# Normalising and projecting by pairs of row blocks, a new order for the last groups, and one branch less at the end of a differential attention and FFN kernel

## The reference

```python
xn = layernorm(x)                                   # (1, 1024, 256)
# attention: 16 heads, d = 8 for queries and keys, 16 for values, causal
q1, k1, q2, k2, v = split(xn @ Wqkv)                # 128, 128, 128, 128, 256 columns
diff = softmax(q1 k1') v - lam * softmax(q2 k2') v  # lam from four vectors of 8
diff = 0.44.. * diff / sqrt(mean(diff**2) + 1e-5)   # per head and row
attn = diff.reshape(...) @ Wproj
# FFN, operands cast to fp8, results bf16
ffn = fp8(gelu(fp8(xn) @ fp8(Wg[0])) * (fp8(xn) @ fp8(Wg[1]))) @ fp8(Wlin)   # hidden 1024
return x + attn + ffn
```

## Time and profile before

| what | us |
|---|---|
| median of 3 runs (lowest, highest) | 199.3 (198.45, 199.69) |
| the profiled execution | 199.27 |
| its span, first to last instruction | 197.5 |
| first exponential starts | 38.0 |
| last exponential starts | 178.9 |
| last product with the values ends (the transpose behind it starts) | 182.9 |
| last block of the output copied by VectorE | 190.4 |

### The profile page before, as it was taken

One profiled execution on the slowest core, in us unless ns is written; L12 is line 12 of the kernel. 1 busy time (PEld: TensorE's weight loads), 2 busy tenths in 40 slices (PEclk: granted clock), 3 DMA queues, 4 the chain that ended last, 5 costly groups with the idle time before them and its releaser, 6 DMA issues.

```text
span 197.5 us, 3554 instructions
## 1 busy us (share of the span) xinstructions
PE 182.2 (92%) x1446; PEld 78.3 (40%) x1450; DVE 92.4 (47%) x218; ACT 163.6 (83%) x136; POOL 59.4 (30%) x71
## 2 busy tenths in 40 slices
PE   6899989899999999999989999999998999899940
PEld 6855334454332323242333424344342423233830
DVE  0975798431223240540472025216703697895840
ACT  2156865899999999999999999999999899998010
POOL 8526600042216142314442043235216124320000
PEclk9999999999999999999999999999999999999997
DMA  5967377780000000000277781000000000000051
GB/s 174 404 242 245 73 179 205 207 190 10 0 0 3 0 0 3 0 0 3 60 203 188 181 191 39 0 3 0 0 3 0 0 3 0 0 3 0 0 178 44
DMA packets 8149, 14.99 MB, mean 76 GB/s; under 512 B 1984, under 2 KB 5312, under 8 KB 8128
## 3 DMA queue, kind: packets, MB, share of 16 engines
q1 hardware_dynamic: 7440, 14.05, 25.5%
q10 hardware_dynamic: 688, 0.66, 1.0%
HBM read 5.26 MB, written 1.05 MB: 32 GB/s over the span
## 4 chain that ended last, share of the span: by engine, by line
PE 74%; ACT 15%; DVE 4%; POOL 1%; issue 1%; POOLq 0%; DVEq 0%
PE ps L910 29%; PE ps L898 17%; ACT probs L442 13%; PE ps L752 8%; PE ps L758 4%; PE ps L941 4%; PE ps L747 3%; PE ps L851 3%; PE ps L813 3%; DVE area L529 2%; DVE o_t L594 1%; ACT probs L430 1%; PE ps L742 1%; PE ps L947 1%; ACT L430 1%
## 5 line engine op out<-in xcount | busy, mean ns | idle before, releaser
L442 ACT ACTIVATE probs<-ps,shift 128x1536 f32<-128x1536 f32 x96 | 140.1, 1554 | 2.4 <-PE ps L898 1.6
L910 PE MATMUL ps<-probs,v_all 128*32 128x512 f32 (+3 forms) x768 | 78.1, 496 | 1.5 <-DVE o_t L594 1.5
L366 POOL TENSOR_SCALAR_AFFINE_SELECT probs<-probs 128x1024 f32<-128x1024 f32 (+1 forms) x40 | 36.7, 917 | 109.7 <-ACT probs L442 109.6
L898 PE MATMUL ps<-q_st,k_st 32*128 32x512 f32 (+3 forms) x384 | 49.8, 420 | 1.2 <-issue 0.8
L898 PEld LDWEIGHTS ps<-q_st,k_st 32*128 32x128 f32 x384 | 22.4, 182 | 58.6 <-ACT probs L442 30.4
L594 DVE STREAM_TRANSPOSE o_t<-ps 128x512 f32<-128x512 f32 x16 | 11.5, 717 | 49.5 <-PE ps L910 49.5
L910 PEld LDWEIGHTS ps<-probs,v_all 128*32 128x32 f32 x768 | 16.4, 108 | 19.6 <-issue 13.9
L752 PE MATMUL ps<-xn_t,w_q 128*128 128x512 f32 (+1 forms) x38 | 17.3, 557 | 0.8 <-ACT xn_t L393 0.8
L813 PE MATMUL ps<-area 128*128 128x512 fp8e4 x64 | 14.5, 379 | 1.0 <-DVE area L529 1.0
L430 ACT ACTIVATE probs<-ps 128x512 bf16<-128x512 f32 x16 | 9.3, 597 | 4.5 <-PE ps L813 2.7
L529 DVE TENSOR_TENSOR area<-ps,probs 128x512 fp8e4<-128x512 f32 x16 | 10.5, 687 | 1.8 <-ACT probs L430 1.7
(11 more groups left out here) (78 smaller groups left out, 117.2 us busy)
## 6 DMA issues: line engine op xcount, KB each, us to landing
q_st<-parts SPq DMA_DIRECT2D x32, 128.0 KB, 2.8
k_st<-parts SPq DMA_DIRECT2D x32, 128.0 KB, 2.8
probs<-L_ffn_w_gating SPq DMA_DIRECT2D x4, 512.0 KB, 7.8
probs<-L_ffn_w_linear SPq DMA_DIRECT2D x1, 1024.0 KB, 13.1
w_q<-L_attn_Wqkv SPq DMA_DIRECT2D x2, 384.0 KB, 5.8
out<-probs SPq DMA_DIRECT2D x3, 256.0 KB, 3.0
x_sb<-L_attn_x SPq DMA_DIRECT2D x2, 256.0 KB, 4.2
x_sb<-L_attn_x ACTq DMA_DIRECT2D x2, 256.0 KB, 4.5
```

The source lines that it names most:

```text
L366: pool.affine_select(out=blocks, in_=blocks, pattern=pattern, compare_op=ALU.is_ge, fill=0.0, base=0, channel_multiplier=-1).then_inc(mask ...
L442: act.activation(probs[:, at:at + PER_UNIT, :].rearrange("p s u -> p (s u)"), ps[:, 3 * (n % 2):3 * (n % 2) + 3, :].rearrange("p b n -> p ...
L898: ins = pe.matmul(ps[:, bank, at:at + wide * P], k_st[rows, g % STACKS, kb * P:(kb + 1) * P], q_st[rows, g % STACKS, queries], start=True, ...
L910: ins = pe.matmul(ps[32 * j:32 * j + 32, 6, q0 % HALF:q0 % HALF + wide * P], v_all[:, g % HG, kb, 32 * j:32 * j + 32], probs[:, slot + j, ...
```

## The change

1. **Start.** `stats_of`, `root`, `transposes` and `turned` work on pairs of blocks, four times. Of each pair VectorE normalises the even block and ScalarE the odd one (`odd_block`). A pair is transposed into one bank. TensorE's order is: pair 0; half of unit 0; pair 1; half of unit 1; the other halves of units 0 and 1; pair 2; values of block 0; pair 3; values of block 1; first norms; unit 2 and so on. WARM_UP is unchanged.
2. **Chunks.** Chunks 5 and 6 change places, so that the masked one is complete two units earlier.
3. **Lateness.** `due` uses 5 for groups 0 to 4, 4 for group 5, 3 for group 6; for group 7 it uses 3, and 2 from chunk 6 on. Before: 5 for groups 0 to 5, 4 for group 6, 3 or (chunks 5 to 8) 2 for group 7.
4. **Second FFN layer.** Block 2 moves to slot 53, block 3 to slots 56 and 57, block 4 to slot 61, and the others one slot ahead.
5. **Output projection.** project(0, 0) and project(1, 0) move from slot 94 to slots 83 and 87. `ending` begins with a wait for out_t_ready 3 and project(0, 1) and (1, 1), ahead of chunks 7 and 8; then blocks 2 and 3 whole, and the first halves of 4 to 7 ahead of the wait for out_t_ready 4. The Y_BANK table follows; blocks 4 and 5 share a bank, and VectorE adds their residual.
6. **VectorE's order.** `take` stands by itself and is placed ahead of other work; `inverse_root` comes in pieces of 64, 32, 16 and 16 columns; the first `down` is ahead of the last `keep`. ScalarE loads the table for the square root by a small operation behind the last exponential, and copies blocks 2, 3 and 6.
7. **Branches.** The flag of the second branch is 0 or 2; the general second branch exists once on TensorE, and behind second_branch(False) one jump is left.

```diff
-    [(1, 4, 512)], [(7, 1, 896), (5, 3, 640)], [(2, 4, 512)], [(3, 4, 512)],
+    [(7, 1, 896), (5, 3, 640)], [(1, 4, 512)], [(2, 4, 512)], [(3, 4, 512)],
...
-DIAGONALS = {0: [0], 1: [0, 128], 2: [0, 256], 4: [0], 6: [0, 128]}
+DIAGONALS = {0: [0], 1: [0, 128], 2: [0, 256], 4: [0], 5: [0, 128]}
...
-DOWN_AT = {44: (0, 0, 4), 45: (0, 4, 8), 49: (1, 0, 8), 56: (2, 0, 4), 57: (2, 4, 8), 61: (3, 0, 8), 65: (4, 0, 8),
-           68: (5, 0, 4), 69: (5, 4, 8), 73: (6, 0, 8), 79: (7, 0, 4), 80: (7, 4, 8)}
+DOWN_AT = {44: (0, 0, 4), 45: (0, 4, 8), 49: (1, 0, 8), 53: (2, 0, 8), 56: (3, 0, 4), 57: (3, 4, 8), 61: (4, 0, 8),
+           67: (5, 0, 4), 68: (5, 4, 8), 72: (6, 0, 8), 78: (7, 0, 4), 79: (7, 4, 8)}
+
+Y_AT = {83: 0, 87: 1}
...
+    late = (5, 5, 5, 5, 5, 4, 3, (3, 3, 3, 3, 3, 3, 2, 2)[min(c, 7)])[g]
     return g * STEPS + last_unit(c) + late
...
             root(0)
+            odd_block(0)
+            root(1)
             turned(0)
-            root(1)
+            odd_block(1)
+            root(2)
+            turned(1)
+            odd_block(2)
+            root(3)
             upper(0)
+            odd_block(3)
+            upper(1)
+            turned(2)
             square_of(0)
-            upper(1)
-            turned(1)
+            turned(3)
...
-            down(0)
+            take(4, 0)
             own.step(difference(0, 0))
             down(1)
+            take(4, 1)
             own.step(difference(0, 1))
+            take(5, 0)
             own.step(difference(1, 0))
             down(2)
+            take(5, 1)
             own.step(difference(1, 1))
-            own.step(difference(2, 0))
+            take(6, 0)
+            inverse_root(slice(0, 64))
             down(3)
-            inverse_root(slice(0, 64))
             scale_by_root(0, all_of)
             scale_by_root(1, all_of)
             turn_back(0, 0)
             turn_back(0, 1)
+            own.step(difference(2, 0))
+            take(6, 1)
             own.step(difference(2, 1))
+            inverse_root(slice(64, 96))
+            take(7, 0)
+            scale_by_root(2, all_of)
             own.step(difference(3, 0))
-            inverse_root(slice(64, 112))
-            scale_by_root(2, all_of)
+            inverse_root(slice(96, 112))
             scale_by_root(3, first)
             turn_back(1, 0)
+            add(0)
+            take(7, 1)
             difference(3, 1).then_inc(ms_ready, 1)
...
             transposes(0)
             pe.wait_ge(wq_in, 32)
-            unit(0)
-            unit(1)
-            transposes(1)
+
+            for i in range(2):
+                pe.wait_ge(xt_out, i + 1)
+                for u in range(2):
+                    for k in range(KC):
+                        ins = queries_keys(u, QK_BANK[u], k, i * C, C)
+                    if i == 1:
+                        ins.then_inc(qk_ready, 1)
+                    elif u == 0:
+                        transposes(1)
+            transposes(2)
+            project_values(0, 6)
+            transposes(3)
+            project_values(1, 6)
...
             def ending():
 
+                pe.wait_ge(out_t_ready, 3)
+                project(0, 1)
+                project(1, 1).then_inc(y_ready, 1)
                 values_due(UNITS, 0, GROUPS)
+                values_due(UNITS + 1, 0, GROUPS)
+                pe.wait_ge(res_ready, TB // 2)
                 for b in (2, 3):
                     project(b, 0)
-                values_due(UNITS + 1, 0, GROUPS)
-                pe.wait_ge(out_t_ready, 3)
-                for b in range(4):
-                    project(b, 1)
-                pe.wait_ge(res_ready, TB // 2)
-                for b in range(4, TB):
+                    residual(b)
+                    project(b, 1).then_inc(y_ready, 1)
+                for b in (4, 5, 7, 6):
                     project(b, 0)
-                    residual(b)
+                residual(6)
                 pe.wait_ge(out_t_ready, 4)
-                for b in range(4, TB):
-                    project(b, 1)
+                project(4, 1)
+                for b in (5, 6, 7):
+                    project(b, 1).then_inc(y_ready, 1)
...
+            pe.reg_load(mode, flag[0:1, 0:1])
+            with pe.If_eq(mode, 0):
                 attention(0, False)
                 pe.wait_ge(flag_ready, 2)
...
+                pe.reg_load(mode, flag[0:1, 1:2])
+                with pe.If_eq(mode, 0):
                     second_branch(False)
...
+            with pe.If_ne(mode, 0):
+                with pe.If_eq(mode, 1):
+                    attention(0, True)
+                    pe.wait_ge(flag_ready, 2)
+                    pe.reg_load(mode, flag[0:1, 1:2])
+                    with pe.If_eq(mode, 0):
+                        second_branch(False)
+                with pe.If_eq(mode, 2):
                     second_branch(True)
```

More of the change, by code:

```diff
@@ L298, in _ @@
             sp.wait_ge(flag_ready, 2)
-            large2 = sp.value_load(flag[0:1, 1:2], min_val=0, max_val=1)
-            with sp.If(large2 == 1):
+            large2 = sp.value_load(flag[0:1, 1:2], min_val=0, max_val=2)
+            with sp.If(large2 == 2):
                 sp.wait_ge(max_split[1], 1)
@@ L385, in _, with root, odd_block, turned @@
                 act.dma_start(x_sb[:, b:b + 2, :], x_rows[:, b:b + 2, :]).then_inc(x_in[b // 2], 16)
[L386 to L394, removed]
+            def root(i):
+                act.wait_ge(var_ready, i + 1)
+                act.activation(rstd[:, 1, 2 * i:2 * i + 2], rstd[:, 0, 2 * i:2 * i + 2], ACT.Sqrt).then_inc(root_ready, 1)
+            def odd_block(i):
+                b = 2 * i + 1
+                act.wait_ge(moved_ready, i + 1)
+                act.activation(xn[:, b, :], x_sb[:, b, :], ACT.Identity, bias=rstd[:, 3, b:b + 1],
+                               scale=rstd[:, 2, b:b + 1]).then_inc(odd_ready, 1)
+            def turned(i):
+                act.wait_ge(xt_ready, i + 1)
+                act.activation(xn_t[:, :, i * C:(i + 1) * C], ps[:, i, :].rearrange("p (k n) -> p k n", k=KC), ACT.Copy
+                               ).then_inc(xt_out, 1)
             def upper(u):
@@ L608, in difference @@
                 b, s = slice(16 * h, 16 * h + 16), slice(32 * i + 16 * h, 32 * i + 16 * h + 16)
-                take(HG + i, h)
                 divide(HG + i, h)
@@ L687, in _ @@
             keep(3, 0)
-            keep(3, 1)
             dve.wait_ge(flag_ready, 2)
-            with dve.If(dve.value_load(flag[0:1, 1:2], min_val=0, max_val=1) == 1):
+            large2 = dve.value_load(flag[0:1, 1:2], min_val=0, max_val=2)
+            steps = own.n
+            with dve.If(large2 == 2):
+                keep(3, 1)
                 maxima(1)
+                down(0)
+            own.n = steps
+            with dve.If(large2 == 0):
+                down(0)
+                keep(3, 1)
             def add(b):
                 dve.wait_ge(res_ready, b // 2 + 1)
-                dve.wait_ge(y_ready, b // 2 + 1)
+                dve.wait_ge(y_ready, {0: 0, 4: 3}[b] + 1)
                 dve.tensor_tensor(y[:, b:b + 2, :].rearrange("p b c -> p (b c)"), ps[:, Y_BANK[b], :],
@@ L736, in _, with transposes @@
             pe.wait_ge(ident_set, 1)
-            def transposes(h):
-                for b in range(4 * h, 4 * h + 4):
-                    pe.wait_ge(xn_ready, b + 1)
+            def transposes(i):
+                for e in range(2):
+                    pe.wait_ge((even_ready, odd_ready)[e], i + 1)
                     for k in range(KC):
-                        ins = pe.transpose(ps[:, 2 * h + k, (b % 4) * P:(b % 4 + 1) * P],
-                                           xn[:, b, k * P:(k + 1) * P], ident[:, :])
+                        ins = pe.transpose(ps[:, i, k * C + e * P:k * C + (e + 1) * P],
+                                           xn[:, 2 * i + e, k * P:(k + 1) * P], ident[:, :])
                 ins.then_inc(xt_ready, 1)
@@ L937, in project @@
             def project(b, p):
[L939 to L944 removed]
+                at = b % 2 * C if b in (0, 1, 4, 5) else 0
+                return pe.matmul(ps[:, Y_BANK[b], at:at + C], out_t[:, p, b * P:(b + 1) * P], w_p[:, p, :],
+                                 start=(p == 0 and at == 0), stop=(p == 1), skip_group_check=True)
             def residual(b):
```

132 lines of the change are left out of this document (58 added, 74 removed).

## The result

The changed kernel takes 200.85 us (median of 16) against 199.12 (median of 16): ratio 1.0084, 95% interval 1.0061 to 1.0107. It is 1.7 us slower, where I forecast 1.2 us faster. One of the 16 executions is left out of the ratio because it was disturbed. The profiled execution took 199.87 us, span 197.8, so it is one of the faster ones; against the profile of before (199.27, 197.5) it is 0.3 longer in span.

| stretch (us) | before | after | difference |
|---|---|---|---|
| start of the span to first exponential | 38.0 | 37.7 | -0.3 |
| exponential 0 to 48 | 72.1 | 72.1 | 0.0 |
| 48 to 69 | 30.0 | 31.4 | +1.4 |
| 69 to 84 | 22.5 | 23.4 | +0.9 |
| 84 to 95 | 16.4 | 19.1 | +2.7 |

The account below looks back on a forecast made before the run. TensorE and ScalarE were taken as nearly level through the attention, with the tail hanging on one chain. The terms, 0 + 1.3 + 0.5 + 0.8 - 3.8 = -1.2 us, gave 198.1 us from 199.3, range 195.8 to 201.0.

Parts of the forecast that it names:

- Term 1: Start, up to the first exponential: statistics by pairs change nothing, 0 us (bounds -0.3 and +0.3).
- Term 2: Slots 48 to 69: filling slot 53 loses TensorE's lead, neighbouring groups add a wait; +1.3 us (0.7 to 1.5).
- Term 3: Slots 83 to 95: double slot removed -0.7, slot 83 stall +0.7, slot 91 wait +0.5; +0.5 us (-0.7 to +1.7).
- Term 4: Ending: TensorE waits for out_t_ready 3 ahead of chunks 7 and 8, +0.8 us (0.2 to 1.3).
- Term 5: Behind the last product: one jump fewer and output written earlier, -3.8 us (-2.9 to -4.4).
- Rival C: TensorE's end: one jump costs what two did because it covers the same code; 201.9 us, chance 0.09.
- Rival B: Slots 83, 91 and ending: VectorE falls behind in series, each wait at its upper end; 200.9 us, chance 0.13.
- Rivals A and D: A: VectorE keeps up from slot 83, 196.3 us, chance 0.25; D: start gains 1 us, 197.1 us, chance 0.08.
- my three signs of being wrong: TensorE's lead survives slot 53; VectorE's operations are not stretched; the fetch is not what held the last write.

Follow-up runs that it names:

- late_as_before: Changed kernel with inverse_root of 48 columns in one piece, chunk 7 ahead of the ending's wait, parts 3 and 4 undone, project(0, 0) and (1, 0) in slots 94, 95: 195.57 us.
- start_down_first: The kernel before with part 1 (start by pairs) and VectorE's down(0) placed ahead of keep(3, 1): 199.04 us, ratio 0.9997.
- start_only: The kernel before with part 1 alone (statistics, normalisation and first projections by pairs): 200.54 us, ratio 1.0064.
- take_ahead: The changed kernel with take(7, 0) ahead of inverse_root of columns 64 to 96: 201.98 us, ratio 1.0132 against the kernel before.
- one_inverse: The changed kernel with one inverse_root of 48 columns behind difference(3, 0) instead of pieces of 32 and 16: 197.07 us, ratio 0.9891 against the kernel before.

## Why the prediction was wrong

**Term 1, the start: right.** Start 37.7 against 38.0 is not the change. In the twelve profiles of this study the granted clock goes to 2.4 GHz for the first time between 4.5 and 7.7 us of the span, and the first exponential follows it: 36.99 with 4.53, 37.73 with 6.07, 38.48 with 7.65 in kernels with the new start. The kernel before has 38.01 with 6.93, late_as_before, with the new start, 38.11 with 6.88. The warm-up matmuls show why: they come 0.21 us apart before the rise and 0.11 behind it, so a late rise delays TensorE's first real work. start_down_first, equal to before in time, settles that the new order gives nothing. What I did not see is that VectorE's jump becomes slow with it and costs 1.3 us if it is not covered (start_only).

**Term 2, slots 48 to 69: right.** +1.4 against +1.3, with the waits where I put them (steps of 2.03 at 65 and 1.98 at 76); late_as_before takes it back, without the wait at slot 65.

**Term 3, slots 83 to 95: this is the step that failed.** I had it at +0.5 with an upper bound of +1.7; exponential 69 to 95 took 3.6 us longer. The removed double slot gave its 0.7, slot 83 cost 1.0 (0.7 forecast; out_t_ready 2 came 7.9 us behind the take of group 6, as in my sum with masks). The rest is slot 91: 3.3 us against 0.5. "Up to 1.5 us late with three; TensorE's regained lead covers half" was wrong in two ways. VectorE was 2.0 us late (176.07 against 174.0, the end of the chunk), and the wait alone cost 1.8 (estimate above): difference(2, 1) took 3.75 us and not 2.35, since masks beside it stretched two steps, and inverse_root 2.84 and not 2.45, with one step of 0.60 instead of 0.19 beside a mask. And I had no term for the clock, which cost the other 1.5: 2.8 us idle went with 3.4 us at 1.2 GHz. take_ahead and one_inverse show both: with the take in time, either the same lack of VectorE's time comes out in the ending, and the lower clock with it, or both are gone with eleven operations less.

**Term 4, the wait ahead of chunks 7 and 8: wrong in this kernel.** +0.8 forecast, 0.0 measured from the last exponential to the last take. From the end of take(7, 0) VectorE needed 7.1 us, as in my sum with masks (7.2), but TensorE came to the ending 7.8 us behind it and not 6.1, most of the difference being the lower clock of slots 91 and 92 (6.4 in one_inverse, at 2.4 GHz throughout). So out_t_ready 3 came in time. In one_inverse the wait is there, 1.33 us, and adds 0.8 up to the last take. That this is my number is luck: VectorE's chain there is another, 7.7 us with inverse_root of 48 columns in it. In take_ahead, with my two pieces, it is 3.67.

**Term 5, the tail: right, a little too small.** -3.8 forecast, -4.5 measured. One jump costs what I took, 3.7; the last write landed 9.8 us behind the last product, 0.5 sooner than I had put it, and the span ended 0.7 sooner. Rival C fell: a first jump costs 3.4 to 3.7, also over the long code, and one directly behind it 5.1 to 5.6. That the fetch held the last write, on which part of the term rests, fits the packets but was not isolated. The rule of the Trainium skill (page "Runtime: NRT & Kernel Launch", section Instruction fetch mechanics) that a taken branch out of the window waits for a fetch agrees with these, and VectorE's jumps of 2.8 and 3.5 us fit it too.

**Rivals and signs.** Rival B had the mechanism (VectorE's take of (7, 0) more than 1 us late decides), but I gave it 0.13 and took 0.5 of the 1.5 us that I had counted with masks, though they lie one behind another: GpSimd was busy for 3.68 of the 4 us from 168 to 172. That B's 200.9 is the measured median is luck: it had 1.7 for term 3 (measured 3.6), 1.3 for term 4 (0.0) and -2.9 for term 5 (-4.5), and its 1.5 was the upper end of term 2, not of a wait named there. Rivals A and D fell: VectorE did not keep up, and the start gave nothing. Of my three signs of being wrong, the first two did not come up and the third stays open; none of them was the clock.

**The whole.** In the profiles, terms 2 to 4 sum to +5.1 up to the last take where I had +2.6, and the tail gave 4.5. Why the median moved by 1.7 and the profiles by only 0.6 is the open clock question above.

## To carry over

An engine's chain in which each link is on time by itself can still be short of time in sum: add its work between two points that another engine waits for, with the stretching by neighbours, before splitting it into more and smaller operations (here 22 instead of 11, some 2 us). Moving a wait does not help while the sum stays; making the sum smaller gave 3.8 us. Ask also what a wait of TensorE does to its clock: here 1.5 of the 3.3 us. And look at the sequencers' rows at the end and at jumps: the slow ones took 2.8 to 5.6 us here, and whether that counts depends on what stands beside it. TensorE's second jump was worth 1.9 us in one kernel and 3 to 4 in the other, and VectorE's 1.3 us in one place and nothing in another.

## What was not expected of the hardware

- TensorE's granted clock fell to 1.2 GHz at idle times of 2.83 us (four profiles) and 3.67 us (one), for 3.4 and 6.8 us, though it had been at 2.4 GHz for over 170 us; at idle times of 1.33 us (slot 83, ending of one_inverse) it did not. The fall came between 0.9 us before and 0.7 us after TensorE went on.
- The first rise to 2.4 GHz came at 5.95 to 7.65 us in three profiles of one kernel (the changed one) and at 4.5 to 7.7 us in all twelve; the first exponential moved with it, by 0.8 and by 1.5 us. Single profiles are best compared from the first exponential on.
- Four recorded instructions more in VectorE's program (251 against 247), all ahead of the first exponential, went with a jump of 2.8 us where it had been 0.5. In start_only an instruction packet of 8 KB runs at 119.97, between the jump and VectorE's going on at 121.78; in the kernel before it comes at 120.29, with down(0) at work since 119.66. That the place of the jump's target decides it is argued from this pair; no run moved the target alone.
